# Gated delta net: the triangle inverse kept in one orientation, with the 16x16 back substitution placed elsewhere in the order of work

## What is computed

```python
attn = -(einsum('bhcid,bhcjd->bhcij', k_beta, k) * decay_mask)   # strictly lower triangle
attn, _ = lax.scan(_correct_row, attn, arange(1, 64))            # row by row
attn = attn + eye                                                # = inverse of (I - lower)
value_corrected = attn @ v_beta
k_cumdecay = attn @ (k_beta * g_exp)
# then chunk by chunk, with the state carried:
v_prime = v_c - kcd_c @ state
out = (q_c @ state) * ge_c + intra @ v_prime
state = state * gel_c + (k_c * kd_c)^T @ v_prime
```

## Time and profile before

| | |
|---|---|
| median of 3 runs | 3184.04 us |
| the profiled execution, its own time | 3190.36 us |
| its span (first to last instruction) | 3188.6 us |
| mean granted TensorE clock | 0.869 of 2.4 GHz |
| TensorE matmuls busy | 2620.2 us (82%) |
| VectorE busy | 1616.2 us (51%) |
| ScalarE busy | 1142.0 us (36%) |
| GpSimd busy | 438.4 us (14%) |
| the delta net's heads, about | 980 to 2780 us |
| from one head's first `z` to the next's, in TensorE's timeline | 117.15 us (1766.71 to 1883.86) |

### The profile page before, as it was taken

How to read it: one execution, slowest core, us unless ns; L and a number is a source line. 1 busy time by engine, 2 the same in 40 slices (tenths; PEclk the granted TensorE clock), 3 DMA queues, 4 the chain that set the end, 5 groups by cost and what they waited for, 6 DMA issues and landing times. The chain is left out here.

```text
span 3188.6 us, 60191 instructions
## 1 busy us (share of the span) xinstructions
PE 2620.2 (82%) x23890; PEld 1999.5 (63%) x23890; DVE 1616.2 (51%) x3376; ACT 1142.0 (36%) x2442; POOL 438.4 (14%) x479
## 2 busy tenths in 40 slices
PE   7899879999656778778778778777877877789998
PEld 4433559999534556556557556556655656679997
DVE  4443456766244445445455454454454544466663
ACT  1123222332134345445444444444444444323221
POOL 0011000000011122122122222222212212100000
PEclk9889889999768789789788788788888878889999
DMA  1000112010011110110110110010011000011110
GB/s 44 25 1 1 30 41 77 27 52 26 5 34 27 27 25 15 28 28 8 28 28 8 28 28 12 24 28 16 22 30 25 11 21 12 19 66 53 44 35 13
DMA packets 172725, 85.22 MB, mean 27 GB/s; under 512 B 121664, under 2 KB 162128, under 8 KB 172496
## 3 DMA queue, kind: packets, MB, share of 16 engines
q1 hardware_dynamic: 172496, 82.02, 9.8%
HBM read 74.51 MB, written 7.47 MB: 26 GB/s over the span
## 5 line engine op out<-in xcount | busy, mean ns | idle before, releaser
L1431 PE MATMUL dn_ps<-xnT,dn_w 128*128 128x512 f32 x512 | 298.9, 721 | 60.1 <-DMA dn_w<-in_W_qkvz_dram 41.0
L435 ACT ACTIVATE g_h<-g_ps,g_b_now 128x512 f32<-128x512 f32 x256 | 174.9, 688 | 338.4 <-PE g_ps L459 332.5
L472 PE MATMUL g_ps<-g_w_low,g_h_high 128*128 128x256 f32 x1024 | 289.8, 283 | 0.0
L472 PE MATMUL g_ps<-g_w_high,g_h_low 128*128 128x256 f32 x1024 | 289.8, 283 | 0.0
L472 PE MATMUL g_ps<-g_w_high,g_h_high 128*128 128x256 f32 x1024 | 289.7, 283 | 0.0
L1804 DVE SCALAR_TENSOR_TENSOR dn_cv<-dn_raw,dn_cw,dn_cv 128x1024 f32<-128x1024 f32 x192 | 282.3, 1470 | 5.3
L1758 POOL TENSOR_TENSOR xn<-xn,dn_zt 128x256 f32<-128x256 f32 x128 | 99.3, 776 | 1198.5 <-DVE xn L1898 856.9
L1871 DVE TENSOR_TENSOR dn_zi<-dn_ps,dn_mz 128x128 f32<-128x128 f32 x256 | 66.5, 286 | 312.4 <-PE dn_ps L1504 308.1
L459 PE MATMUL g_ps<-g_x_high,g_w_high 128*128 128x512 f32 x512 | 201.9, 394 | 17.8 <-DVE g_w_low L516 15.6
L1489 PE MATMUL dn_ps<-ident,dn_bi 64*64 64x64 f32 x1024 | 58.0, 270 | 179.1 <-POOL dn_bi L1746 174.2
L1431 PEld LDWEIGHTS dn_ps<-xnT,dn_w 128*128 128x128 f32 x512 | 103.7, 221 | 161.6 <-issue 128.2
(11 more groups left out here) (270 smaller groups left out, 5482.7 us busy)
## 6 DMA issues: line engine op xcount, KB each, us to landing
g_w<-in_fc_dram SPq DMA_DIRECT2D x32, 1024.0 KB, 6.4
dn_w<-in_W_qkvz_dram SPq DMA_DIRECT2D x16, 768.0 KB, 4.4
dn_x<-dn_cum_rows SPq DMA_DIRECT2D x32, 256.0 KB, 3.9
dn_wout<-in_W_out_dram SPq DMA_DIRECT2D x16, 256.0 KB, 2.8
f_gate<-in_gateT_dram SPq DMA_DIRECT2D x16, 128.0 KB, 2.2
f_up<-in_upT_dram SPq DMA_DIRECT2D x16, 128.0 KB, 2.3
f_down<-in_downT_dram SPq DMA_DIRECT2D x16, 128.0 KB, 2.5
dn_blocks_rows<-dn_ge SPq DMA_DIRECT2D x128, 16.0 KB, 1.7
```

What stands on the lines that cost most here:

```text
L435: nc.scalar.activation(h[:, f % 4], h_b[f % 4], ACT.Gelu, bias=b1_now[u // 2][:, f:f + 1]).then_inc(h_ready, 1)
L472: last = pe.matmul(y_b[q % 2][:, 0:D], hidden[:, f, q * P:(q + 1) * P], weights[:, f, :], start=(f == 0 and n == 0), stop=(f == NF - 1 and ...
L1431: mm = pe.matmul(to, w[:, k, W_COL[u] * P:(W_COL[u] + 1) * P], m.xnT[:, k, b * T:(b + 1) * T], start=(k == 0), stop=(k == KD - 1))
```

## The change

In words, with the places:

- The lower factor is no longer transposed. `unit` is one GpSimd instruction for a whole head that adds the identity to `ge` in place, behind `spread`'s stores; `lower`, `bi`, `ai`, `AI_r`, `D0_r` and `BI_r` are gone, on TensorE, ScalarE and GpSimd. `z` multiplies `ge` itself with the transposed inverse, `e` the other way round, and the masks (`mz`) are transposed. The number of multiplications in `z` and `e` is as before.
- `base` works on `inverse`, now only a transposed view of `turned`. The copy L1864 is gone. The waits stand before each instruction instead of behind it.
- `gather` stores and reads back `turned` alone: one store and 8 loads. `w16` is made from `w16t` by a new step, `mirror`: one VectorE transpose of 128x1024 (32x32 blocks).
- The order: `base`, in four pieces with nothing between them, then `gather` and `unit` stand at the very end of the second pair, behind the four taps of input 3. `mirror` stands at the end of the third pair. In the second pair `proj` 6 moves to the first slot, the four `gram` and `decay` steps go two by two into the second and third slot with `spread` behind them, `silu` v0 into the fourth, and `proj` 7 stays in the fifth.

The diff, cut to its core:

```diff
-    for size in (2, 4, 8, 16, 32, 64):
+    for size in (2 * BASE, 4 * BASE):
...
-        off = (pair[:, None] == pair[None, :]) & low[None, :] & ~low[:, None]
+        off = (pair[:, None] == pair[None, :]) & low[:, None] & ~low[None, :]
...
-    yield from [("base", j), ("gather", j)]
+    yield from [("base", j, n) for n in range(4)] + [("gather", j), ("unit", j), ("mirror", j)]
 
 
 def front_order(j, c):
-    yield from [("turn", j, c), ("turn", j, c + 1), ("unit", j, c), ("unit", j, c + 1), ("lower", j, c)]
+    yield from [("turn", j, c), ("turn", j, c + 1)]
...
     yield from ahead(1, "turn")
-    yield from ahead(0, "unit")
-    yield from ahead(1, "unit")
     yield from extra[5]
-    yield from ahead(0, "lower")
     yield from extra[6]
...
+        BS = lambda n: [("base", q, n)] if prep else []
...
-            GD(0), GD(2), SL("v0") + GD(4), GD(6) + ONE("spread"), PR(6) + PR(7), TP(3, 0, 1), TP(3, 2, 3)])
+            PR(6), GD(0) + GD(2), GD(4) + GD(6) + ONE("spread"), SL("v0"), PR(7), TP(3, 0, 1), TP(3, 2, 3) + BS(0) + BS(1) + BS(2) + BS(3) + ONE("gather") + ONE("unit")])
         yield from pair_order((j, 4), (j, 6), (q, 0) if prep else None, [
-            SL("v1"), PR(8), PR(9), ONE("base") + ONE("gather") + PR(10), PR(11), [], []])
+            SL("v1"), PR(8), PR(9), PR(10), PR(11), [], ONE("mirror")])
...
+        inverse = turned[:].rearrange("p s r -> p r s")
...
-                    for tile, scratch in ((inverse, inverse_dram), (turned, turned_dram)):
-                        sp.dma_start(scratch.rearrange("h t n r s -> (h t n) (r s)"), tile[:].rearrange("p r s -> p (r s)")).then_inc(w16_stored, 16)
-                    sp.wait_ge(w16_stored, (kh + 1) * 32)
+                    sp.dma_start(turned_dram.rearrange("h t n r s -> (h t n) (r s)"), turned[:].rearrange("p r s -> p (r s)")).then_inc(w16_stored, 16)
+                    sp.wait_ge(w16_stored, (kh + 1) * 16)
                     wait(sp, "E_r", 16 * (kh - 1))
-                    wait(sp, "z16", 4)
-                    for tile, scratch in ((w16, inverse_dram), (w16t, turned_dram)):
-                        for h in range(GRP):
-                            for t in range(QUARTERS):
-                                rows = slice(h * C + t * BASE, h * C + (t + 1) * BASE)
-                                sp.dma_start(tile[f][rows, :, t * BASE:(t + 1) * BASE],
-                                             scratch[h, t].rearrange("n r s -> r n s")).then_inc(w16_loaded, 16)
+                    wait(sp, "z16", 2)
+                    for h in range(GRP):
+                        for t in range(QUARTERS):
+                            rows = slice(h * C + t * BASE, h * C + (t + 1) * BASE)
+                            sp.dma_start(w16t[f][rows, :, t * BASE:(t + 1) * BASE],
+                                         turned_dram[h, t].rearrange("n r s -> r n s")).then_inc(w16_loaded, 16)
...
-                        wait(pe, "AI_r", i * 8 + so_far["lower"])
...
-                elif name == "lower":
-
-                    c, = a
-                    wait(pe, "A_e", i * 16 + so_far["turn"])
-                    wait(pe, "ev", i * 24 + so_far["proj"])
-                    wait(pe, "BI_r", chunk(i, j, c) + 2)
-                    for n in range(2):
-                        for b in range(B):
-                            for h in range(GRP):
-                                mm = pe.matmul(block_of(bA, n, b, h), bi[n][half(h), b, :], eye_of(h), start=True, stop=True)
-                    mm.then_inc(s_["D0_r"], 1)
                 elif name == "z":
                     c, l = a
                     s = c % 2
                     f = j % 2
                     if l == 0:
-                        wait(pe, "AI_r", pair_count(i, j, c) + 1)
-                        pe.wait_ge(w16_loaded, (kh + 1) * 32 * GRP * QUARTERS)
+                        wait(pe, "G_r", kh + 1)
+                        pe.wait_ge(w16_loaded, (kh + 1) * 16 * GRP * QUARTERS)
                         wait(pe, "WT_r", level(i, j, c, 0) - 1)
                     else:
                         wait(pe, "WT_r", level(i, j, c, l - 1) + 1)
-                    inverse_of = wt[s][:, 0] if l else of_chunk(w16[f], c)
+                    turned_of = wt[s][:, 1] if l else of_chunk(w16t[f], c)
                     for b in range(B):
                         for h in range(GRP):
-                            mm = pe.matmul(block_of(bD[s], 0, b, h), ai[half(h), s, b, :], inverse_of[half(h), b, :], start=True, stop=True)
+                            mm = pe.matmul(block_of(bD[s], 0, b, h), of_chunk(ge[f], c)[half(h), b, :], turned_of[half(h), b, :],
+                                           start=True, stop=True)
                     mm.then_inc(s_["Z_r"], 1)
                 elif name == "e":
                     c, l = a
                     s = c % 2
-                    turned_of = wt[s][:, 1] if l else of_chunk(w16t[j % 2], c)
+                    inverse_of = wt[s][:, 0] if l else of_chunk(w16[j % 2], c)
                     wait(pe, "Zi_r", level(i, j, c, l) + 1)
+                    if l == 0:
+                        wait(pe, "mirror_r", kh + 1)
                     for b in range(B):
                         for h in range(GRP):
-                            mm = pe.matmul(block_of(bD[s], 1, b, h), turned_of[half(h), b, :], zi[s][half(h), b, :], start=True, stop=True)
+                            mm = pe.matmul(block_of(bD[s], 1, b, h), zi[s][half(h), b, :], inverse_of[half(h), b, :], start=True, stop=True)
                     if l < LEVELS - 1:
                         for b in range(B):
                             for h in range(GRP):
-                                mm = pe.matmul(block_of(bD[s], 2, b, h), zi[s][half(h), b, :], turned_of[half(h), b, :],
+                                mm = pe.matmul(block_of(bD[s], 2, b, h), inverse_of[half(h), b, :], zi[s][half(h), b, :],
                                                start=True, stop=True)
                     mm.then_inc(s_["E_r"], 1)
...
-                elif name == "lower":
-                    c, = a
-                    wait(act, "D0_r", pair_count(i, j, c) + 1)
-                    wait(act, "Z_r", level(i, j, c, 0))
-                    copy(ai[:], bA[:, 0:2 * P].rearrange("p (s b n) -> p s b n", s=2, b=B)).then_inc(s_["AI_r"], 1)
...
-                    s, n = c % 2, chunk(i, j, c)
-                    wait(pool, "C_e", pair_count(i, j, c) + 1)
-                    wait(pool, "D0_r", pair_count(i, j, c))
-                    nc.gpsimd.tensor_tensor(bi[s][:], of_chunk(ge[f], c), over_b(eye2), ALU.add).then_inc(s_["BI_r"], 1)
+                    wait(pool, "C_e", kh * 4 + 4)
+                    pool.wait_ge(ge_stored, (kh + 1) * 16 * GRP * QUARTERS)
+                    nc.gpsimd.tensor_tensor(ge[f][:], ge[f][:], over_head(eye2), ALU.add).then_inc(s_["G_r"], 1)
...
-            for tile in w16 + w16t:
+            for tile in w16t:
...
-                    wait(dve, "BI_r", chunk(i, j, 0) - 8)
+                    wait(dve, "Z_r", 16 * (kh - 1))
...
-                    links_of_base = 2 * (BASE - 2) + 1
-                    made = [kh * links_of_base]
+                    stage, = a
+                    rows = BASE - 2
+                    bounds = [rows, rows - 3, rows - 7, rows - 11, 0]
+                    made = [kh * (2 * rows) + (1 + 2 * (rows - bounds[stage]) if stage else 0)]
 
                     def then(instruction):
                         instruction.then_inc(s_["base_c"], 1)
                         made[0] += 1
-                        wait(dve, "base_c", made[0])
-
-                    dve.wait_ge(blocks_loaded, (kh + 1) * 16)
-                    dve.wait_ge(w16_stored, kh * 32)
-                    then(nc.vector.tensor_tensor(inverse[:], whole_blocks[:], eye16[:], ALU.add))
-                    for t in range(BASE - 2, 0, -1):
+
+                    if stage == 0:
+                        dve.wait_ge(blocks_loaded, (kh + 1) * 16)
+                        dve.wait_ge(w16_stored, kh * 16)
+                        then(nc.vector.tensor_tensor(inverse, whole_blocks[:], eye16[:], ALU.add))
+                    for t in range(bounds[stage], bounds[stage + 1], -1):
                         n = BASE - 1 - t
                         products = outer[:, 0:t * n].rearrange("p (r n) -> p r n", r=t)
                         above = inverse[:, 0:t, t + 1:BASE]
+                        wait(dve, "base_c", made[0])
                         then(nc.vector.tensor_tensor(products, whole_blocks[:, 0:t, t:t + 1].broadcast_to([P, t, n]),
                                                      inverse[:, t:t + 1, t + 1:BASE].broadcast_to([P, t, n]), ALU.mult))
-                        then(nc.vector.tensor_tensor(above, above, products, ALU.add))
-                    nc.vector.tensor_copy(turned[:].rearrange("p s r -> p r s"), inverse[:]).then_inc(s_["base_r"], 1)
+                        wait(dve, "base_c", made[0])
```

(10 more changed lines are left out.)

28 lines of the change are left out of this document (12 added, 16 removed).

## The result

| | before | after |
|---|---|---|
| median of 4 runs | 3183.82 us | 3130.43 us (3129.93 to 3133.89) |
| the profiled execution | 3190.36 us | 3129.93 us |
| its span | 3188.6 us | 3128.2 us |
| mean granted TensorE clock | 0.869 | 0.891 |
| TensorE matmuls busy | 2620.2 us | 2504.8 us |

The account below looks back on a forecast made before the run. TensorE's order was taken to bound the kernel, with idle time before `lower` (174.2 us) and `z` (93.2 us). Terms summed to -2.75 us a head, -41 over 15 heads, -8.5 at the ends: 3184 - 50 = 3134 us, range 3085 to 3205.

Parts of the forecast that it names:

- A: Likeliest case: gather and `dn_w` won, VectorE's block at the second pair's end costs two thirds; 3134 us, chance 0.55.
- End of the first pair: `lower` and its wait go, but `new_values` still waits for `dn_wv` behind VectorE's taps: -0.4 us a head.
- Second pair: Adjacent grams wait for `decay`, one projection less and one gram more behind the first `new_values`: +1.4 us a head.
- The clock there: Second pair: TensorE's slow stretch after the new idle time falls on work that counts; +1.2 us, bounds 0 to 1.9.
- rival C: Slower: idle stretches and gram gaps keep TensorE at 1.2 GHz through much of second and third pair; 3209 us, chance 0.17.
- End of the second pair: Base block now stands ahead of `dn_wv`, +7.05 us; GpSimd's `unit` and `dn_kept` block VectorE's taps, +2.1 us a head.
- Third pair: A slow clock stretch after some 13 us without TensorE work lies wholly behind `new_values`: +1.4 us, bounds 0 and 1.9.
- End of the third pair: `lower` goes, the gather is early, and the projection waits only for `dn_w`, about 1 us: -15.4 us a head.
- `mirror`: VectorE transpose ahead of the third pair's end `dn_wv`: 1.23 us at no cost; at 2.81 it costs 1.1.
- The ends: Outside the steady heads: -3.5 us in the prologue before the first `z`, -5 us in the last head.
- Rival B: The clock terms (2.6) and GpSimd's blocking (2.1) don't count: -7.4 us a head, 3064 to 3100 us, chance 0.2.
- D: Rival: `z` still waits, for `mirror`, `unit` or SP, keeping 6.2 us idle; +3.45 a head, 3227 us, chance 0.03.

Follow-up runs that it names:

- e8: Changed kernel with dummy TensorE multiplications, 2 us in the second pair's first slot and six times as many in the third's: 3133.59 us, ratio 0.983.
- e4: Changed kernel with only the second pair's first five slots in the old order, grams one to a slot: 3088.76 us, ratio 0.969.
- e6: Changed kernel with `inverse` a tile of its own again, copied into `turned` at the end of base: 3116.19 us, ratio 0.978.
- e3b: Changed kernel with `unit` moved behind the third pair's first `update`, whose GpSimd part waits for VectorE: 3129.6 us, ratio 0.981.
- e1: Changed kernel with the old order of the second and third pair, `unit` at the end of the second: 3180.76 us, ratio 0.997.
- e5: Changed kernel with a second transpose of `mirror`'s size ahead of it, into a tile nobody reads: 3140.32 us, ratio 0.986.
- e2: Changed kernel with base and gather one slot later, in the third pair's first slot behind `silu` v1: 3000.39 us, ratio 0.940.
- e3: Changed kernel with `unit` moved from the second pair's end to the third pair's second slot: 3138.72 us, ratio 0.984.
- e10: Changed kernel, old gram order, base/gather and `unit` in the third pair, own `inverse` tile, fills of 2 and 4 us: 2947.05 us, ratio 0.925.

## Why the prediction was right, point by point

The time was right (3134 for 3130) and so was the likeliest case, A: the gather and `dn_w` are won, and the block of VectorE costs most of it. Two errors of some 2 us a head cancel in it, and that is luck. The steps against one head (1807.7 of before, 1779.0 of after):

- **End of the first pair**, -0.4: 8.56 to 7.79, -0.8. Some small VectorE instructions in front of the taps are shorter there, now that GpSimd's additions into `bi` are gone. `new_values` waits 2.36 us, as forecast 2.4.
- **Second pair**, +1.4 for the grams: the waits behind `decay` came as forecast, 0.90, 0.91 and 0.28. They add up to 2.1; mine, 0.8, 0.8 and 0.4, add up to 2.0, and I had carried 2.2. **The clock there, +1.2: this is the term that was mis-sized.** The pair rose by 4.7, not 2.6. e8 shows how that divides: with the grams paired and the clock full it is 14.8, so the order of the grams costs 2.0 and the clock 2.6. With the grams back in e4 it is 14.2, of which the clock has 1.5. I had bounded the clock's part by 0 to 1.9. The slow stretch that I had it from was 3.4 us long; the new one is 6.8, from 1802.9 to 1809.7. So the bound holds for the idle time alone, as e4 shows, and was wrong in its upper end for an idle time with the waits of paired grams behind it. The mechanism of rival C was therefore at work, with some 2 us beyond my terms in this pair, where it decides from 2.75 a head. The clock of the whole pair is 0.80, not near 0.5.
- **End of the second pair**, +7.05 and +2.1: 8.85 to 18.05, +9.2 for 9.15. The base is dearer than thought (7.74 us from 1828.53 to 1836.27 for 7.05, through the view; e6), the taps cost 1.8 for 2.1 (6.55 for 4.74 us; e3b gives 1.95 of it back). The wait at `dn_wv` is 14.36, above the 12 to 13 forecast and within the 9 to 15 that I had given.
- **Third pair**, +1.4: 14.40 to 15.05 in that head, +0.7; against the mean of before, 1.1. The slow stretch behind the wait lasts 3.5 us, not 3.7 to 5.6, against 1.9 behind `new_values` before: half of the difference is 0.8.
- **End of the third pair**, -15.4: 22.04 to 6.52, -15.5. `dn_w` waits 1.08 for about 1. e1 shows that most of it came from the place: with the old place the gain here is 4.0 of 14.7 in the mean, from the shorter relay and the missing `lower`.
- **`mirror`**: 1234 ns for 1.23, at no cost (e5). The Trainium skill's figure for a VectorE transpose (VectorE: DVE Perf Modes, "The three transpose paths"), 311 ns for 128x128 in bf16, had given an estimate of 2.5 us for eight; the trace does not agree with scaling it by eight.
- **Fourth and first pair**, 0: -0.4 and -1.6. Not forecast. In the heads shown the projection behind the norms takes 1.98 us where it took 3.38, and the output's first eight multiplications 3.00 for 3.62: slow stretches stood here before and now stand in the second pair. Together this is 2.0, and cancels the 2.1 of the second pair.
- **The wait for `xn`**, called "late next at the same time": yes, 4.80 for 3.13 and 0.64 with `lower` between them.
- **The ends**: the stretch from the net's first projection to the first `z` fell from 70.66 to 67.04 us, -3.6 for -3.5, and from the last of the 15 heads to the end of the span 6.2 us went, for 5. From that first `z` to the first head's `new_values` another 3.5 went (20.35 to 16.88), not forecast. The profiled execution of before was 6 us above its median; 3 us of the difference lie in front of the delta net, where nothing was changed.
- **The sum**: -3.8 in this head, -3.2 in the mean and 44.3 us in 15 heads, for -2.75 and 41. From one head's `z` to the next's it is 112.65 us (1742.17 to 1854.82), for about 114.5; the 117.15 of before that I started from was 1.6 above its mean head.

Rival B is excluded by the second pair and by the taps, D by `z` without a wait. That the change's place of the base might be pure loss was my idea after the result, and e1 refuted it: the place is what relieves the relay. But e2 shows a third place, one slot later, that relieves it as well and costs almost nothing. It lies three slots ahead of the old one. The prediction weighed only the two places that the change names.

What stays open is what sets the length of a head to the last microsecond once the waits are known; see the last section.

## What to carry to other kernels

Look for a block's place between two deadlines: the latest start that its DMA relay allows, and the first small instruction behind it in its engine's queue that the main engine waits for. Here one slot later, behind that instruction, was worth 7.8 of the 9.5 us by which that stretch had grown, and the slot that feeds the relay too late left a gain of 0.3%. A step moved in a list moves on an engine only if something there makes it wait; and a gain of a few us in one stage can be taken back in another by the clock's slow stretches, as 1.95 us were in e3b and 2.6 in e8, though not the 3.2 of e4: so check it over whole loop rounds, not in the stage where it was made.

## What the runs showed of the hardware that I had not expected

**The clock takes small gains back.** Kernels with different waits have heads of the same length: 112.6 us in the changed kernel, e3 and e5, and in e3b with 1.95 us less at the end of the second pair. The lengths that heads repeat stand some 3 to 4 us apart: 98.8 to 99.2, 102.4 to 102.8, 105.5 to 105.7, 109.1 to 109.6, 112.3 to 112.9, 115.8 to 116.3. Of the 143 heads of the means outside e8 and e10, 10 lie elsewhere; where TensorE was filled, most do (111.8 and 113.5 in e8, 99.3 to 102.4 in e10). Within one kernel, what makes up the difference is mostly how much of the first and the second pair runs at the low clock: the first is 14.7, 16.3 or 17.8, and the second, with the grams in pairs, 14.8 or 17.4. In the traces the slow stretches follow idle ones, but not each idle one at the same distance. No run here settles why.

**Stride.** A float32 VectorE instruction of 256 elements a partition took 0.59 us with an output whose elements lie 64 bytes apart and 0.42 with a dense one; the longest product took 0.258 us with one operand like that and 0.219 with dense ones (e6).

**A later place in the list isn't a later time.** `unit`, one pair later in the list, ran at the same place (e3).
